# Opening stage and two queues of a fused AdaLN block: gate row, cosines, modulation rows, spills and last tile in another order

## The reference

```python
mod = (silu(c) @ wmod).reshape(2, 6, 1, -1)            # c: 2 x 512, wmod: 512 x 3072
sa, ca, ga, sb, cb, gb = (mod[:, i] for i in range(6))
ga = sign(ga) * maximum(abs(ga), 0.25)                  # gb likewise
h = layernorm(x) * (1 + ca) + sa
x = x + ga * attention(h, wq, wk, wv, wo)               # 32 query heads, 8 kv heads of 128, rope, causal window of 128
h = layernorm(x) * (1 + cb) + sb
x = x + gb * ffn(h, w12, b12, w3, b3)                   # silu(x1) * x2, both of width 512
```

## Time and profile before

| | |
|---|---|
| median of 3 runs | 1507.73 us (1504.65 to 1507.94) |
| profiled execution | 1505.94 us, its span 1504.1 us |
| PE busy | 1476.1 us, 98% of the span |
| DVE, POOL, ACT busy | 1103.5, 868.4, 823.2 us |
| mean granted PE clock | 0.995 of 2.4 GHz |

### The profile page before, as it was taken

How to read it: one execution, slowest core, us unless ns; L and a number is a source line. 1 busy time by engine, 2 the same in 40 slices (tenths; PEclk the granted TensorE clock), 3 DMA queues, 4 the chain that set the end, 5 groups by cost and what they waited for, 6 DMA issues and landing times.

```text
span 1504.1 us, 27328 instructions
## 1 busy us (share of the span) xinstructions
PE 1476.1 (98%) x7577; PEld 1227.3 (82%) x7577; DVE 1103.5 (73%) x1849; ACT 823.2 (55%) x2183; POOL 868.4 (58%) x894
## 2 busy tenths in 40 slices
PE   6989999999999999999999999999999999999998
PEld 4578888888888888887888888888888888877887
DVE  6678787778787878788777878787877868773542
ACT  3555565656555656555565655565655556552331
POOL 2346565556565566669855656556664665675333
PEclk9999999999999999999999999999999999999999
DMA  9011110020201111324302020111111101153001
GB/s 315 21 36 57 36 56 28 18 73 7 72 18 56 35 56 35 104 71 134 106 16 77 7 70 21 56 35 56 35 56 35 56 28 38 60 182 127 28 29 56
DMA packets 98688, 90.20 MB, mean 60 GB/s; under 512 B 5450, under 2 KB 73042, under 8 KB 98646
## 3 DMA queue, kind: packets, MB, share of 16 engines
q1 hardware_dynamic: 97718, 87.06, 18.4%
q0 software_dynamic: 640, 2.10, 0.4%
q10 hardware_dynamic: 288, 0.53, 0.1%
HBM read 74.98 MB, written 14.69 MB: 60 GB/s over the span
## 4 chain that ended last, share of the span: by engine, by line
PE 87%; issue 4%; DVE 4%; POOL 3%; ACT 1%; DMA 1%; SPq 0%; POOLq 0%; DVEq 0%; ACTq 0%
PE pP L276 11%; PE pP L278 11%; PE pP L277 11%; PE pOp L276 8%; PE pOp L278 7%; PE pOp L277 7%; PE pS L278 4%; PE pAv L276 4%; PE pS L277 4%; PE pS L276 4%; PE pAv L277 4%; PE pAv L278 4%; PE pTr L286 3%; PE pXx L355 1%; POOL y L1310 1%
## 5 line engine op out<-in xcount | busy, mean ns | idle before, releaser
L1242 POOL TENSOR_SCALAR_AFFINE_SELECT pm<-pT 128x512 fp32r<-128x512 f32 x480 | 392.3, 850 | 477.8 <-DVE pT L865 477.7
L276 PE MATMUL pP<-hT,wp 128*128 128x512 f32 (+1 forms) x776 | 314.5, 405 | 6.9 <-DVE hT L998 4.0
L278 PE MATMUL pP<-hT,wp 128*128 128x512 f32 (+1 forms) x776 | 303.3, 391 | 0.0
L277 PE MATMUL pP<-hT,wp 128*128 128x512 f32 (+1 forms) x776 | 302.3, 390 | 0.0
L629 ACT CAST oT<-pAv 128x512 fp32r<-128x512 f32 x128 | 74.9, 585 | 283.8 <-PE pAv L278 283.8
L1255 POOL TENSOR_TENSOR rB<-rB,tab 128x512 f32<-128x512 f32 x160 | 218.3, 1376 | 16.3 <-ACT rB L652 16.2
L641 ACT ACTIVATE pr<-pS,nb 128x128 f32<-128x128 f32 x512 | 181.4, 371 | 63.3 <-DVE nb L885 63.2
L895 DVE TENSOR_TENSOR rA<-pP,tab 128x512 f32<-128x512 f32 x160 | 110.3, 689 | 131.0 <-ACT rB L652 131.0
L276 PE MATMUL pOp<-wos,oT 128*128 128x512 f32 x512 | 201.4, 393 | 3.7 <-DVE oT L860 3.4
L278 PE MATMUL pOp<-wos,oT 128*128 128x512 f32 x512 | 199.6, 390 | 0.0
L277 PE MATMUL pOp<-wos,oT 128*128 128x512 f32 x512 | 199.3, 389 | 0.0
(11 more groups left out here) (187 smaller groups left out, 3016.1 us busy)
## 6 DMA issues: line engine op xcount, KB each, us to landing
st<-in_L_attn_wq_dram SPq DMA_DIRECT2D x64, 256.0 KB, 3.5
st<-in_L_attn_wo_dram SPq DMA_DIRECT2D x64, 256.0 KB, 3.7
h_dram<-hs SPq DMA_DIRECT2D x16, 512.0 KB, 3.9
st<-in_L_attn_wk_dram SPq DMA_DIRECT2D x16, 256.0 KB, 4.2
st<-in_L_attn_wv_dram SPq DMA_DIRECT2D x16, 256.0 KB, 2.6
wm<-in_L_wmod_dram SPq DMA_DIRECT2D x4, 1024.0 KB, 10.2
xin<-in_L_attn_x_dram SPq DMA_DIRECT2D x16, 256.0 KB, 3.1
qT<-h_dram SPq DMA_DIRECT2D x2, 2048.0 KB, 10.2
```

Source lines behind the costliest of these rows:

```text
L276: nc.tensor.matmul(o, hi_l, hi_r, start=start, stop=False, skip_group_check=True)
L277: nc.tensor.matmul(o, hi_l, lo_r, start=False, stop=False, skip_group_check=True)
L278: return nc.tensor.matmul(o, lo_l, hi_r, start=False, stop=stop, skip_group_check=True)
L1242: last = nc.gpsimd.affine_select(out=pm[:, own, part], in_=pT[:, part], compare_op=op, fill=0.0, base=0, pattern=[[0, G], [sign, P]], chan ...
```

## The change

Five edits. Row 1 of `mod` directly follows row 0 on PE, and its copy on ACT stands ahead of the two weight casts. On DVE the cosine products stand ahead of the statistics and norms of tiles 6 and 7. The first gate is made one unit sooner on DVE. Six of the eight spills are issued by SP in place of POOL. The last tile is computed, gated, added and stored in two halves of 256 columns; DVE makes its residual add in place of POOL, and ACT's queue stores the second half.

```diff
@@ tensor
             mod_row(0)
+            mod_row(1)
             first_transpose(0)
             first_transpose(1)
             mod_columns(0)
-            mod_row(1)
             first_transpose(2)
...
-                o = [pOp, pXx][i % 2]
...
+                for n in ((slice(0, 256), slice(256, 512)) if i == 15 else (slice(0, 512),)):
+                    o = pP0 if n.start else [pOp, pXx][i % 2]
+                    for m in range(4):
+                        last = mm3(o[:, n], x4[:, 0, m, t * P:(t + 1) * P], x4[:, 1, m, t * P:(t + 1) * P],
+                                   wp[:, 0, m, n], wp[:, 1, m, n], m == 0, m == 3)
+                    last.then_inc(f_out, 1)
@@ scalar
             row_copy(0, 0)
+            row_copy(1, 1)
             split_weight(f0, wp[:, 0, 0, :], 0, 0)
             split_weight(f0, wp[:, 0, 1, :], 1, 1)
-            row_copy(1, 1)
...
+            act.wait_ge(f_last, 2)
+            act.dma_start(out[1, 7 * P:8 * P, 256:512], st[:, 0, 256:512]).then_inc(s_store[0], 16)
@@ vector
             for i in range(5):
                 rope_cos(f0, 0, i)
+                if i:
+                    rope_sum(f0, i - 1, i)
+                if i in (3, 4):
+                    ln_apply(3 + i)
                 if i < 3:
                     split_first(3 + i)
                 if i:
                     rope_lo(f0, names[i - 1], 0, i - 1, i)
-                if i < 2:
-                    ln_stats(6 + i)
-                rope_sum(f0, i, i + 1)
-                if i < 2:
-                    ln_apply(6 + i)
+                if i in (2, 3):
+                    ln_stats(4 + i)
+            rope_sum(f0, 4, 5)
...
                     if (b, u) == (0, 0):
+                        gate_row(0)
                         mod_out(2)
                         mod_out(3)
                     if (b, u) == (0, 1):
-                        gate_row(0)
                         gate_row(1)
...
+            dve.wait_ge(s_store[0], 48)
+            for h in range(2):
+                n = slice(256 * h, 256 * h + 256)
+                dve.wait_ge(f_out, 16 + h)
+                nc.vector.tensor_tensor(st[:, 0, n], [pXx, pP0][h][:, n], bc[:, 1, 1, n], ALU.mult).then_inc(f_gated, 1)
+                dve.wait_ge(f_gated, 16 + h)
+                dve.wait_ge(f_resb, 16)
+                nc.vector.tensor_tensor(st[:, 0, n], st[:, 0, n], x1_tile(15)[:, n], ALU.add).then_inc(f_last, 1)
@@ gpsimd
-                if j < 2:
-                    ln_rstd(6 + j)
+                if j in (2, 3):
+                    ln_rstd(4 + j)
...
-                        spill(u + 5)
+                        if u == 1:
+                            spill(6)
...
-                    if b == 0 and u >= 3:
-                        spill(u - 3)
@@ sync
+            def spill(t):
+
+                sp.wait_ge(s_fin, t + 1)
+                sp.dma_start(x1_spill[t * P:(t + 1) * P, :], y[:, t, :]).then_inc(s_spill[t], 16)
...
-                    load_x(2), load_x(3)
+                    load_x(2)
+                    spill(0)
+                    load_x(3)
+                    spill(1)
...
+            sp.wait_ge(f_last, 1)
+            sp.dma_start(out[1, 7 * P:8 * P, 0:256], st[:, 0, 0:256]).then_inc(s_store[0], 16)
```

More of the change, by code:

```diff
@@ L193, in adaln_block @@
         x1_in = [sem(f"x1_in{i}") for i in range(2)]
-        f_pe, f_silu, f_x4, f_hi, f_lo, f_out, f_gated, f_res, f_resb = (sem(n) for n in (
-            "f_pe", "f_silu", "f_x4", "f_hi", "f_lo", "f_out", "f_gated", "f_res", "f_resb"))
+        f_pe, f_silu, f_x4, f_hi, f_lo, f_out, f_gated, f_res, f_resb, f_last = (sem(n) for n in (
+            "f_pe", "f_silu", "f_x4", "f_hi", "f_lo", "f_out", "f_gated", "f_res", "f_resb", "f_last"))
         s_store = [sem(f"s_store{i}") for i in range(5)]
@@ L1226, in _ @@
                     ff_gate(i - 4)
-            for i in range(12, 16):
+            for i in range(12, 15):
                 ff_gate(i)
+            dve.wait_ge(s_store[0], 48)
[6 more added lines that the diff above has]
+                nc.vector.tensor_tensor(st[:, 0, n], st[:, 0, n], x1_tile(15)[:, n], ALU.add).then_inc(f_last, 1)
         @block.gpsimd
@@ L1515, in _ @@
                     load_h(hT[:, :, :, CT:CT + 3 * P], 0, 1, (4, 5, 6))
-                    load_x(4), load_x(5)
+                    load_x(4)
+                    spill(2)
+                    load_x(5)
+                    spill(3)
                     store_side(f, 0, NKV - 1)
                     load_h(hT[:, :, :, CT + 3 * P:SEQ], 0, 1, (7,))
-                    load_x(6), load_x(7)
+                    load_x(6)
+                    spill(4)
+                    load_x(7)
+                    spill(5)
             for i in range(12):
@@ L1554, in _ @@
             sp.dma_start(x1b[:], x1_spill[CT:2 * CT, :].rearrange("(t p) d -> p t d", p=P)).then_inc(x1_in[1], 16)
-            for i in range(2 * NT):
+            for i in range(2 * NT - 1):
                 sp.wait_ge(f_res, i + 1)
@@ L1558, in _ @@
                              ).then_inc(s_store[i % 5], 16)
+            sp.wait_ge(f_last, 1)
+            sp.dma_start(out[1, 7 * P:8 * P, 0:256], st[:, 0, 0:256]).then_inc(s_store[0], 16)
             for i in range(5):
-                sp.wait_ge(s_store[i], 16 * ((2 * NT - i + 4) // 5))
+                sp.wait_ge(s_store[i], 16 * (5 if i == 0 else 3))
 _INS = ["L0_attn_x", "L0_attn_wq", "L0_attn_wk", "L0_attn_wv", "L0_attn_wo", "L0_ffn_w12", "L0_ffn_b12", "L0_ffn_w3",
```

## The result

The changed kernel takes 1498.15 us as the median of 5 runs (1497.24 to 1499.11), the kernel before 1507.17 us in 5 runs on the same chip. The ratio is 0.9947, with a 95% interval of 0.9932 to 0.9961: 8.0 us faster, between 5.9 and 10.2 (the two medians differ by 9.0). The two profiled spans differ by 6.8 us, 1504.1 against 1497.3. The forecast was 1501.0 us, with a range of 1497.0 to 1505.5.

The account below looks back on a forecast made before the run. PE, busy 98% of the span, was taken as the bound. Terms 0.0 - 4.8 - 0.4 - 0.9 = -6.1 us gave 1499.8 from the profile, 1501.6 from the median; forecast 1501.0 us, range 1497.0 to 1505.5.

Parts of the forecast that it names:

- Row 1 behind row 0: Opening: `modT` starts near 16.95 rather than 18.47, 1.5 us sooner, bounds 1.0 to 2.2.
- the same half clock behind it: K and Q0 projections: they move up 1.5 us with the 4 us wait and half clock behind it unchanged.
- Cosines ahead of norms: Opening: Q2's 1.8 us wait goes, a 3.9 us wait comes before V, V at half clock loses 1.4 to 1.7.
- The opening as a whole: Row 1's 1.5 us against V's half-clock loss: 0.0 us; bounds 1.7 sooner to 2.5 later.
- half of the 3.3 us at half clock behind the 1.8 us wait: Behind the wait ahead of Q2's projection: PE works at 0.50 clock, so 1.7 us are lost.
- The gate: First gate's DVE operations hidden in `nb`'s hold: unit 4's scores 4.8 us sooner; bounds 1.4 to 6.1.
- the end of its low part of Q3: DVE work that unit 4's scores need: ends at 96.5, allowance included, rather than 101.1.
- the allowance of 0.3 us: DVE behind the second gate: 0.3 us added for two sums that now meet POOL's masks.
- wait of about 1.3 us: PE near 95 us: a new short wait of about 1.3 us, with DVE late on Q3's low part.
- Rival 2: Gate operations not hidden, third held by clearings until 72.3: gate gains 1.4 or less, about 1505.5 us; chance 0.17.
- Spills on SP's queue: Stretch from 660 to 760 us: POOL loses six issues, 0.4 us sooner; bounds 1.0 sooner, 0.5 later.
- The last tile: Tail: PE ends 0.16 us later, halves and ACT's store end the span 0.9 us sooner; bounds 0.4 to 1.2.

Follow-up runs that it names:

- gate alone: Kernel before with only the first gate's three DVE operations moved from unit 1 to unit 0: 1502.17 us, ratio 0.9968.
- row alone: Kernel before with only row 1 of mod placed right behind row 0: 1506.40 us, ratio 0.9996.
- cosines alone: Kernel before with only the cosine products ahead of tile 6's and 7's norms: 1507.29 us, ratio 1.0002.
- spills alone: Kernel before with only six spills issued by SP in place of POOL: 1507.11 us, ratio 1.0000.
- tail alone: Kernel before with only the last tile in halves, DVE's residual add and the store on ACT's queue: 1506.45 us, ratio 0.9993.
- clearings later: Kernel before with POOL's two clearings of y behind unit 1's work in place of unit 0's: 1503.87 us, ratio 0.9978.
- after, no gate: Changed kernel with the first-gate edit taken out: 1504.23 us, ratio to the kernel before 0.9981.
- after, no cosines: Changed kernel with the old order of cosines and norms: 1497.13 us, ratio to the kernel before 0.9933.
- no cosines, no spills: Changed kernel with only the row, gate and tail edits, cosines and spills as before: 1498.70 us, ratio to the kernel before 0.9946.
- no cosines, clearings later: Changed kernel without its cosine edit and with POOL's two clearings in unit 1 rather than unit 0: 1496.51 us, ratio to the kernel before 0.9930.
- tile 6 behind V: Changed kernel with tile 6's transposes behind V's projection on PE: 1496.89 us, ratio to the kernel before 0.9936.

## Why the prediction held, and where it was off

One pair of profiles can't size terms of 1 us, because stretches at half clock fall differently in each. All 13 profiles together can, cut at the same landmarks: the first write of `modT`, the start of row 5, PE's transposes of the side work near 608 us, SP's first store of `hs` near 1273 us, the end of PE's last matmul and the end of the span. Each number is a difference of two starts (or ends) read from the timelines; the six of a kernel add up to its span.

| kernel | start to `modT` | to row 5 | to 608 | to 1273 | to PE's end | to the span's end |
|---|---|---|---|---|---|---|
| before | 18.47 | 52.99 | 537.08 | 664.92 | 226.13 | 4.51 |
| gate alone | 18.37 | 52.95 | 531.64 | 665.15 | 227.38 | 4.51 |
| row alone | 17.00 | 54.05 | 537.73 | 664.80 | 226.13 | 4.49 |
| cosines alone | 18.50 | 55.39 | 537.61 | 664.94 | 226.09 | 4.47 |
| spills alone | 18.68 | 53.72 | 537.20 | 663.77 | 227.31 | 4.52 |
| tail alone | 18.66 | 54.01 | 537.85 | 665.04 | 226.34 | 3.10 |
| clearings later | 18.34 | 54.03 | 534.53 | 664.82 | 226.11 | 4.47 |
| after | 17.63 | 55.41 | 531.34 | 663.59 | 226.28 | 3.05 |
| after, no gate | 16.68 | 55.04 | 536.38 | 663.36 | 227.54 | 3.10 |
| after, no cosines | 16.51 | 53.85 | 531.58 | 663.45 | 227.57 | 3.14 |
| no cosines, no spills | 17.06 | 53.94 | 531.42 | 665.13 | 226.27 | 3.08 |
| no cosines, clearings later | 16.02 | 53.49 | 531.44 | 664.16 | 226.28 | 3.11 |
| tile 6 behind V | 17.11 | 56.89 | 531.43 | 663.81 | 227.54 | 3.12 |

**Row 1 behind row 0.** Predicted 1.5 us sooner at `modT`. The seven kernels with it reach `modT` at 16.86 on the mean, the six without at 18.50: 1.6. In the pair before and after it was 0.84: row 1 started at 11.28 there, where I had it start at 10.68, though row 0 started at the same time as before (5.01 and 4.97). With row 1 alone it started at 10.64. What the edit fills is a wait that the prediction didn't name, PE's wait for tile 1's norm. PE in the timeline of the kernel before:

```profile
12.56 0.66 PE L377 MATMUL pP<-ident,y 128*128 128x128 f32 x4 [1.22 <-DVE y L974]
```

In the six kernels without the edit row 0 ends between 9.72 and 11.41, this wait of 0.70 to 2.05 us makes up for the difference, and `modT` stays between 18.34 and 18.68. With the edit the wait is gone, `modT` stands 6.35 or 6.36 us behind the start of row 1, and every delay of row 0 goes through: `modT` lies between 16.02 and 17.63. Row 0's matmuls start some 0.85 us apart at first and 0.43 us later. Seven of these gaps are long after the change and three in the kernel with no cosines and later clearings, whose row 1 starts at 9.67. The profile lists a clock of 1.00 there, so why they are long isn't shown.

Part of the 1.6 us seems to be given back in the halves of K and Q0. From K's first matmul to the first swap on ACT it is 5.86 to 6.11 us in the four kernels whose low stretch behind the 4 us wait is 3.4 us long, and 6.67 to 7.34 us in the nine where it is 6.8. All seven kernels with row 1 behind row 0 are among the nine, and two of the six without: 7.05 against 6.36 us on the mean. The prediction has "the same half clock behind it", with a few tenths to either side. That the edit lengthens the low stretch is likely by this count, but not shown.

**Cosines ahead of norms.** Predicted 1.4 to 1.7 us lost, in steps that all came: no wait ahead of Q2's projection, DVE's sums beside POOL's sine products (1.27 us rather than 0.68), a wait of 3.9 us on tile 6's norm (3.94), V at a clock of 0.50. The three kernels that have it with V in place take 55.28 us from `modT` to row 5, the nine without 53.67: 1.6 lost. Finer landmarks show where. From the first swap to V's first matmul it is 16.18 to 16.22 us in eight of the nine kernels with the old order (17.46 in the ninth, the last tile alone) and 15.83 to 16.18 with the new one, where I had V start 0.15 later. From there to row 2 it is 2.91 to 2.94 us with the old order and 4.18, 4.50 and 5.36 with the new one. From row 2 to row 5 it is 23.8 in all twelve. So the loss is V at half clock alone, 1.3 to 2.4 us where I had 1.4 to 1.7, and the longer chain on DVE behind it costs PE nothing.

The opening as a whole comes to about 0.0, as summed: the two kernels with both edits and V in place reach row 5 at 72.4 us on the mean, the five with neither at 72.0. In the profiled pair it is 1.58 us later, which is 0.84 sooner at `modT`, 1.23 lost in the halves of K and Q0, 0.37 sooner at V's start and 1.57 lost in V.

One reading was wrong, though no term of the sum rested on it. I took half of the 3.3 us at half clock behind the 1.8 us wait as time lost. In five kernels the clock stayed up behind that wait, and PE then met a second wait instead. PE in the timeline of row 1 alone:

```profile
35.50 0.47 PE L276 MATMUL pP<-hT,wp 128*128 128x512 f32 x1 [1.81 <-ACT rB L652]
40.85 0.47 PE L276 MATMUL pP<-hT,wp 128*128 128x512 f32 x1 [1.91 <-ACT rB L652]
```

From Q2's projection to Q3's it is 5.35 us at full clock, and it was 5.37 us in the kernel before, most of it at half clock. ACT's swaps set that pace, so the low clock cost nothing.

**The gate.** Predicted 4.8 us sooner. From row 5 to the transpose near 608 us the six kernels with it take 531.48 us on the mean, the six without it (leaving out the later clearings alone) 537.31: 5.8. The mechanism was right at each step: three operations of 0.7 us hidden in the hold of `nb`, scores straight behind row 5, the output projection 6.2 us sooner after a wait of 0.42 (predicted 6.1 and 0.7), no low clock behind it. Mis-sized was the second time that DVE was to be late. I put the end of its low part of Q3 at 96.5 in old times; it ended at 97.30, which is 95.7 in them. It started on this stretch 0.2 us sooner than I had it (84.28, 82.7 in old times, not 82.9), had lost 2.0 us in it to waits for PE and not 1.7 (15.0 us from there to the end of the low part before, 13.0 after), and the allowance of 0.3 us for sums beside POOL's masks wasn't needed. So PE reached unit 4's scores by its own work, at 95.85 in old times, and the wait of about 1.3 us that I expected there isn't there.

The Trainium skill, page "SBUF: State Buffer", section "SBUF: two separate sides", has a DVE operation with two SBUF inputs contend only with a GpSimd operation that reads SBUF. The trace agrees for the gate: L1115 reads `gmag` and `grow` from 71.08 and takes its 0.68 us in the middle of a clearing. Rival 2, that it would be held, is out.

**Spills on SP's queue.** Predicted 0.4 us, at most 1.0. From 608 to 1273 us the six kernels with it take 663.69 us on the mean, the seven without 664.97: 1.3, beyond my upper bound. The step that failed is "PE's whole loss from 660 to 760 is 1.62 us", read as 100 less PE's busy time, with "a good part of it on DVE or POOL's last two spills, which stay". A matmul of 512 columns is shown as 0.39 us while the next starts 0.23 behind it, so the first 0.16 us of each idle time count as busy. Over the 763 equal matmuls PE was busy 145.1 to 145.2 us in the seven kernels with POOL's spills, and 144.4 to 144.5 in the six with SP's. These 0.7 to 0.8 us were waiting time that the busy share hides. The Trainium skill has the general point, page "Perfetto Trace Analysis", section "Identifying the Most-Contended Engine": matmul busy time is a poor measure of how near PE is to its limit, since matmuls are pipelined. That it hides waits, and how much, is from these traces. The weight loads' busy time hardly changed (122.15 us before, 122.34 after).

Where the time went can be seen too. It is one operation of DVE, the low part of the side work's `hs`, whose two inputs lie in SBUF. The list of this line's operations and timelines of DVE, POOL and PE, before:

```profile
L1028 DVE TENSOR_TENSOR hs<-hm,hs x16: 789/800/3304, 135.0 to 1346.6; 128x512 fp32r<-128x512 f32 x16
...
703.25 3.30 DVE L1028 TENSOR_TENSOR hs<-hm,hs 128x512 fp32r<-128x512 f32 x1
...
704.73 1.28 POOL L1287 TENSOR_TENSOR y<-y,bc 128x512 f32<-128x512 f32 x1
...
711.89 0.63 PE L355 MATMUL pXx<-ident,rB 128*128 128x128 f32 x4 [0.38 <-issue]
712.78 0.30 PE L276 MATMUL pS<-kv,qT 128*128 128x64 f32 x1 [0.27 <-DVE qT L912]
```

And after:

```profile
699.03 1.50 DVE L1031 TENSOR_TENSOR hs<-hm,hs 128x512 fp32r<-128x512 f32 x1
...
699.95 1.73 POOL L1301 TENSOR_TENSOR y<-y,bc 128x512 f32<-128x512 f32 x1
...
706.65 0.60 PE L355 MATMUL pXx<-ident,rB 128*128 128x128 f32 x4
```

Before, `hs` ends 0.54 us behind POOL's product with the gate (704.73 + 1.28 = 706.01); after, it ends at 700.53, and it is POOL's product that takes 0.45 us more. All seven kernels with POOL's spills have 3.29 to 3.31 us for this one operation, 94.6 to 94.8 us behind the landmark at 608, and all six with SP's have 1.50 to 1.51. DVE's work behind `hs` comes later for it, and PE meets the two waits shown, which are in all of the seven and in none of the six. The transposes start 103.3 to 103.4 us behind the landmark in the seven and 102.2 to 102.3 in the six. This is 1.1 of the 1.3 us. Why `hs` gets in ahead of that product once POOL has fewer issues to make is not shown.

**The last tile.** Predicted 0.9 us. From PE's end to the span's end it is 3.10 us rather than 4.50, 1.4 less, and the halves cost PE 0.17 us (226.29 against 226.12, where no half clock fell): 1.2. PE's own cost was right (0.16). So were DVE's two operations: they end 0.91 us behind PE's last matmul, for which I had 0.95. The store was shorter than summed: the span ends 2.1 us behind ACT's issue (1495.20), where I had 2.4 to 2.6, near the 2.44 us of the whole tile in the earlier trace rows.

**Sum.** -1.6 + 1.6 - 5.8 - 1.3 - 1.2 = -8.3 us from the traces; the runs say 8.0 [5.9, 10.2]; I had 6.1. The forecast of 1501.0 us was 2.9 too high: 2.2 by the sizes of gate, spills and tile; the other 0.7 is within the scatter of the five runs (1497.24 to 1499.11). The five parts alone add up to 6.2 us by their ratios, but each of those numbers is uncertain by 1.3 to 1.9 us, so that sum tells nothing against the 8.3.

**What stays open.** Putting tile 6 behind V made V start sooner (13.44 us behind the first swap, not 15.83), but in its profile it took 28.98 us from row 2 to row 5 instead of 23.79, with the 1.83 us wait on `qT` and 6.8 us at half clock behind it. Its one profile was taken in the longest of its six runs (1501.6 us). The record has the mean granted clock of each run: 0.994 in this one and in the other above 1501 us, 0.997 to 0.998 in the four between 1495.2 and 1497.2. So most of the 5 us between them is half clock, by its size the stretch behind that wait and the one near 1348 us; that these are the ones missing in the four is not shown. Nor is whether this order is better than that of the change.

## What to carry to other kernels

An operation that is held by another engine is a place to hide work: here 2.1 us of DVE work cost nothing since the next operation could not end before POOL's clearing, and 5.8 us of PE's time came of it. PE's busy share counts short waits as work, so compare the length of a stretch with the same number of matmuls in both kernels, not 100% less the busy share. Look for the one operation whose longest time is far from its median (3304 against 800 ns for `hs`): work that seems unrelated may decide what it has to wait behind. Where PE waits for another engine's pace, work at half clock costs nothing, and closing one wait only moves it: count the time to the next point where PE is not waited for by anybody.

## What the runs showed of the hardware

The stretches at the 1.2 GHz level differ from kernel to kernel, and from one profile to the next where the code before them is the same. Behind the 4.0 us wait ahead of K's projection the granted clock was low for 3.4 us in four profiles and for 6.8 us in nine. Behind the same wait of 4.35 us on the first gate it was low for 3.4 us in one kernel and for 6.8 us in five. Near 1345 us, where PE waits for `oT` twice (3.0 to 3.1 us in all), five of 13 profiles have a low stretch of 3.4 us and eight have none, and it costs 1.25 us (227.5 against 226.2 in the table). This is of the size of the terms that were to be measured.

The second thing is how DVE and POOL hold each other. `nb`, an operation of 128x4 elements, takes 0.17 us once the clearings are moved away. When it begins during POOL's clearing of `y` it takes 2.76, 0.90 or 0.97 us, each time up to the clearing's end, and what stands behind it on DVE ends with it or later. Operations ahead of it that start beside a clearing take their usual time: 0.67 us where they read PSUM, 0.68 us where they read two SBUF tiles. With a POOL product that reads SBUF beside it, an operation with two SBUF inputs is held too: `hs` takes 0.8 us in the median of its line and 1.50 or 3.30 us beside such products.
